# Experts in two halves of the batches, with split matrices kept in DRAM and the first half combined under the second half's tiles

## The reference

```
x = layernorm(x + attention(x))        # 16 heads of 128, 4 groups of K and V, causal
logits = clip(x @ gate_w.T)            # 8 experts
top_w, top_idx = top_k(logits, 2); rw = softmax(top_w)
weighted = (softmax(eaw) @ atoms) * sigmoid(importance)      # 8 x 4096
out = x @ W.T + sum over k of rw[k] * S(weighted[top_idx[k]]) x
x = layernorm(x + out)
```

## Time and profile before

| | us |
|---|---|
| median of 3 runs | 2010.44 (2010.35 to 2011.24) |
| profiled execution, its own time | 2009.37 |
| its span | 2007.8 |
| PE busy | 1830.0 (91%) |
| DVE busy | 1200.9 (60%) |
| POOL busy | 825.7 (41%) |
| ACT busy | 809.5 (40%) |

### The profile page before, as it was taken

One profiled execution on the slowest core, in us unless ns is written; L12 is line 12 of the kernel. 1 busy time (PEld: TensorE's weight loads), 2 busy tenths in 40 slices (PEclk: granted clock), 3 DMA queues, 4 the chain that ended last, 5 costly groups with the idle time before them and its releaser, 6 DMA issues. The chain is left out here.

```text
span 2007.8 us, 35232 instructions
## 1 busy us (share of the span) xinstructions
PE 1830.0 (91%) x9447; PEld 1543.7 (77%) x9448; DVE 1200.9 (60%) x3710; ACT 809.5 (40%) x2038; POOL 825.7 (41%) x1242
## 2 busy tenths in 40 slices
PE   6899999999999999999999999999999824999940
PEld 6788888888888888888888888888888713877730
DVE  4445557775777677667757775777576664222237
ACT  1244434444444444444434443444344353333324
POOL 6266433333342334243324332433333244666633
PEclk9999999999999999999999999999999866999975
DMA  8543353334333433343342334333232152444468
GB/s 306 184 163 132 116 199 107 126 106 139 113 105 105 147 110 120 107 140 110 115 152 94 134 123 145 106 117 123 106 127 74 53 170 93 157 150 153 146 223 358
DMA packets 113038, 278.74 MB, mean 139 GB/s; under 512 B 17809, under 2 KB 28065, under 8 KB 103017
## 3 DMA queue, kind: packets, MB, share of 16 engines
q1 hardware_dynamic: 92128, 229.03, 32.6%
q0 software_dynamic: 20816, 48.73, 7.6%
HBM read 207.00 MB, written 70.72 MB: 138 GB/s over the span
## 5 line engine op out<-in xcount | busy, mean ns | idle before, releaser
L849 POOL TENSOR_SCALAR probs<-probs,row_inv 128x128 f32<-128x128 f32 (+3 forms) x512 | 308.3, 655 | 423.7 <-DVE row_inv L1248 423.1
L1154 ACT ACTIVATE probs<-probs,neg_max 128x512 f32<-128x512 f32 (+3 forms) x512 | 282.2, 553 | 358.4 <-DVE neg_max L1240 356.3
L928 PE MATMUL psum<-xT_hi,w_hi 128*128 128x512 f32 x640 | 253.5, 396 | 6.1 <-PEq L373 3.7
L930 PE MATMUL psum<-xT_hi,w_lo 128*128 128x512 f32 x640 | 251.2, 393 | 0.0
L929 PE MATMUL psum<-xT_lo,w_hi 128*128 128x512 f32 x640 | 250.6, 392 | 0.0
L1240 DVE CUSTOM_DVE_ANT_0 probs<-psum,causal 128x512 f32<-128x512 f32 (+3 forms) x512 | 222.7, 486 | 38.3 <-issue 20.1
L1251 DVE TENSOR_TENSOR pT_lo<-psum,pT_hi 128x512 fp32r<-128x512 f32 (+1 forms) x384 | 206.3, 592 | 21.5 <-ACT pT_hi L1164 21.5
L928 PE MATMUL psum<-wo_hi,oT_hi 128*128 128x512 f32 x512 | 203.3, 397 | 1.5 <-DVE y_acc L1275 0.5
L930 PE MATMUL psum<-wo_hi,oT_lo 128*128 128x512 f32 x512 | 200.4, 391 | 0.0
L929 PE MATMUL psum<-wo_lo,oT_hi 128*128 128x512 f32 x512 | 199.9, 391 | 0.0
L1164 ACT CAST pT_hi<-psum 128x512 fp32r<-128x512 f32 (+1 forms) x384 | 172.4, 526 | 61.0 <-PE psum L955 61.0
(11 more groups left out here) (248 smaller groups left out, 3934.6 us busy)
## 6 DMA issues: line engine op xcount, KB each, us to landing
w_hi<-split_qk_weights SPq DMA_DIRECT2D x140, 256.0 KB, 2.7
w_lo<-split_qk_weights SPq DMA_DIRECT2D x140, 256.0 KB, 2.9
wo_hi<-split_out_weights SPq DMA_DIRECT2D x28, 1024.0 KB, 5.0
wo_lo<-split_out_weights SPq DMA_DIRECT2D x28, 1024.0 KB, 7.0
c_y<-chosen_rows SPq DMA_DIRECT2D x32, 512.0 KB, 9.3
x_in<-in_L_attn_x_dram SPq DMA_DIRECT2D x8, 1024.0 KB, 6.6
expert_weights<-fill_sb SPq DMA_DIRECT2D x4, 2048.0 KB, 9.4
stage<-expert_weights SPq DMA_DIRECT2D x8, 1024.0 KB, 5.3
```

The costliest lines, as they stand in the source:

```text
L849: last = pool.tensor_scalar(p, p, row_inv[:, buf, i:i + 1], 1.0, ALU.mult, ALU.mult)
L928: pe.matmul(dst, hi_s, hi_m, start=start, stop=False)
L930: return pe.matmul(dst, lo_s, hi_m, start=False, stop=stop)
L1154: last = act.activation(probs[:, buf, a:a + w], probs[:, buf, a:a + w], ACT.Exp, bias=neg_max[:, buf, i:i + 1], scale=-1.0, accum_out=row_ ...
```

## The change

- The experts work in two *segments* of four batches (`SEG_B`, `SEG_T` = 16 token tiles), each with its own half of the slot table, its own counts and at most `SEG_TILES` = 39 tiles: 78 tiles in all instead of 72.
- In batches 1 to 4 each iteration scatters twice 128 entries. In batches 5 and 6, two pieces an iteration (16 in all): SP loads 512 KB of `expert_weights`, POOL rounds and subtracts (`split_piece`), and SP writes the hi and lo parts to `split_expert_weights`, expert by expert.
- In batch 7 SP loads the split matrices (2 MB an expert) as parts of attention's buffers come free; the slots of segment 0 are loaded, DVE makes its tables, and POOL fetches the first four tiles. SBUF is laid out by hand (`Space`) so that the buffers may overlap in this way.
- Batch 7's y goes to `attn_residual` like the others, and its four tiles are routed under tiles 0 to 33 of the experts, in seven steps each (`routed`), by the same functions as in attention. Segment 1's tables follow at tiles 29 to 31.
- The 8 pairs of segment 0 are combined under tiles 44 to 76 (`paired`), those of segment 1 behind the last tile. Stores go from SP.
- The gate's rows are loaded by POOL at the end of batch 0. The four iterations of a batch are written out inside the hardware loops, and the 78 tiles without a loop. There are no barriers between attention, experts and combine.

The diff's core:

```diff
+SEGMENTS = 2
+SEG_B = NB // SEGMENTS
+SEG_T = SEG_B * TT
+SEG_TILES = (2 * SEG_T * P + NE * (P - 1)) // P
+JT = SEGMENTS * SEG_TILES
+SCATTER_BATCHES, SPLIT_BATCHES = (1, 5), (5, 7)
...
+    def batch(b, last_kind, route, segment, job):
+        for g in range(HKV):
+            iteration(b, g, b * HKV + g, ("first", "group", "group", last_kind)[g], route, segment, job)
+    batch(0, "batch", False, 0, None)
+    with eng.Fori(*SCATTER_BATCHES) as b:
+        batch(b, "batch", True, 0, "scatter")
+    with eng.Fori(*SPLIT_BATCHES) as b:
+        batch(b, "batch", True, 1, "split")
+    batch(NB - 1, "end", True, 1, "last")
...
+        def load_piece(b, step):
+            src = pieces[bass.ds((b - SPLIT_BATCHES[0]) * 2 + step // PER_C, 1), step % PER_C]
+            sp.dma_start(F.piece_raw[:], src.rearrange("a p n -> (a p) n")).then_inc(s_piece_in, 16)
...
+        def split_piece(b, step):
+            number = piece_number(b, step)
+            raw = F.piece_raw[:].rearrange("p (r e) -> p e r", e=NE)
...
+            pool_round(pool, F.piece_hi[:], raw).then_inc(s_piece, 1)
+            wait_apart(pool, s_piece, 2 * number + 1, s_passed)
+            pool.tensor_tensor(F.piece_lo[:], raw, F.piece_hi[:].bitcast(F32), ALU.subtract).then_inc(s_piece, 1)
...
+                if g == HKV - 1:
+                    sp.wait_ge(s_q, NIT * G)
+                    load_expert(2)
+                    load_expert(3)
+                    sp.wait_ge(s_qk, 3 * NIT * G)
+                    load_expert(4)
+                    sp.wait_ge(s_o, NIT * G)
+                    sp.wait_ge(E.s_tables, 1)
+                    for e in range(5, NE):
+                        load_expert(e)
...
+            if kind != "end":
+                normalize(n + 4, 0)
...
+            if job == "scatter":
+                scatter((it - SCATTER_BATCHES[0] * HKV) * 2 + 1)
...
+            if route:
+                route_place(pool, R, it - TT)
...
+        for j in range(JT):
...
+            if j + GROUP < JT:
+                fetch(pool, R, E, j + GROUP)
+            if j:
+                send(j - 1)
+            tt, step, begun, ranked = routed(j)
+            if ranked and step == 1:
+                route_place(pool, R, tt - 1)
...
+            if begun and step == 2:
+                route_rstd(pool, R, tt)
+            u, step, some = paired(j)
+            if some and step == 2:
+                rstd_of(u)
...
+        add(PAIRS)
+        for v in range(PAIRS_LEFT):
+            u = PAIRS + v
+            spread(u)
+            if v + 1 < PAIRS_LEFT:
+                add(u + 1)
+            variance(u)
+            shift_of(u)
```

More of the change, by code:

```diff
@@ L14 @@
+from collections import namedtuple
 from contextlib import ExitStack
@@ L67, with __init__, __call__ @@
 RAW = HKV
+SCATTER_BATCHES, SPLIT_BATCHES = (1, 5), (5, 7)
+PIECE = P
+PIECES = C * (DM // PIECE)
+PER_C = DM // PIECE
+KB = 1024
+SBUF_FROM, SBUF_TO = 16512, 229344
+class Space:
+    def __init__(self, nc, at, size):
+        self.nc, self.at, self.end = nc, at, at + size
+    def __call__(self, name, shape, dt=F32):
+        size = 4
+        for n in shape[1:]:
+            size *= n
+        tensor = self.nc.alloc_sbuf_tensor_at(name, shape, dt, offset=self.at)
+        self.at += -(-size // 32) * 32
+        assert self.at <= self.end, name
+        return tensor
@@ new lines, in expert_ends, with tiles_behind @@
+def expert_ends(dve, E, t):
+    step = lambda ins: table_step(dve, E, ins)
+    step(dve.tensor_scalar(t.tiles_i[:], t.counts_i[:], P_SHIFT, None, ALU.logical_shift_right))
+    step(dve.tensor_copy(t.tiles[:], t.tiles_i[:]))
+    step(dve.tensor_copy(t.ends[:, 0:1], t.tiles[:, 0:1]))
+    for e in range(1, NE):
+        step(dve.tensor_tensor(t.ends[:, e:e + 1], t.ends[:, e - 1:e], t.tiles[:, e:e + 1], ALU.add))
+def tiles_behind(dve, E, t):
+    step = lambda ins: table_step(dve, E, ins)
+    dve.wait_ge(E.s_tile_at, t.segment + 1)
+    step(dve.tensor_copy(t.tile_at[:], t.tile_at_i[:]))
+    step(dve.tensor_tensor(t.behind[:], t.tile_at[:].unsqueeze(1).broadcast_to([P, NE, SEG_TILES]),
+                           t.ends[:].unsqueeze(2).broadcast_to([P, NE, SEG_TILES]), ALU.is_ge))
+    step(dve.tensor_tensor(t.behind_tiles[:], t.behind[:], t.tiles[:].unsqueeze(2).broadcast_to([P, NE, SEG_TILES]),
+                           ALU.mult))
+    step(dve.tensor_reduce(t.tile_expert[:], t.behind[:].rearrange("p e j -> p j e"), AX.X, ALU.add))
+    step(dve.tensor_reduce(t.tile_start[:], t.behind_tiles[:].rearrange("p e j -> p j e"), AX.X, ALU.add))
@@ L89, in __init__ @@
         self.chosen = sb("route_chosen", [P, 3, NE])
[L90 removed]
+        self.counts = [sb(f"route_counts_{k}", [P, NE]) for k in range(SEGMENTS)]
         self.ranks = sb("route_ranks", [P, NE])
@@ new lines, in build, with _ @@
+        X = experts(sem, s_passed, psum, ident, upper, ones, R, E, tables[1], final, M, y_dram, r_dram, out_rows)
+        with nc.Block() as block:
+            @block.sync
+            def _(sp):
+                M.sync(sp)
+                X.sync(sp)
+            @block.gpsimd
+            def _(pool):
+                M.gpsimd(pool)
+                X.gpsimd(pool)
+            @block.tensor
+            def _(pe):
+                M.tensor(pe)
+                X.tensor(pe)
+            @block.scalar
+            def _(act):
+                M.scalar(act)
+                X.scalar(act)
+            @block.vector
+            def _(dve):
+                M.vector(dve)
+                X.vector(dve)
@@ L310, in route_ranked @@
     wait_apart(dve, R.s_ranks_read, tt + 2, R.passed)
-    step(18, dve.tensor_tensor(R.counts[:], R.counts[:], R.chosen[:, 2], ALU.add))
+    step(18, dve.tensor_tensor(R.counts[segment][:], R.counts[segment][:], R.chosen[:, 2], ALU.add))
     for k in range(2):
```

2130 lines of the change are left out of this document (1029 added, 1101 removed).

## The result

The changed kernel took 1960.4 us (median of 4 runs, 1957.3 to 1967.1) against 2010.4: a ratio of 0.9756, 95% interval 0.9727 to 0.9785. The forecast was 1986, between 1964 and 2006.

What follows compares the result with a forecast made beforehand. It took attention as PE bound and the tiles as POOL bound at 3.42 us each; −13 (attention to last send), −25 (combine) and +14 (attention) sum to −24: span 1984, median 1986 us, range 1964 to 2006.

Steps and rivals of the forecast that it cites:

- A: Stretch from PE's last attention matmul to the last send: 1920.5 against 1933.6 before, so −13 us.
- 73 fetches × 2.12: POOL's row fetches in the tile stage: 155 us of POOL's 278 us of work there.
- When tiles can start: Joint between attention and tiles: expert loads land at 1622, POOL is free for its first send at about 1632.
- B: Combine after the last send: eight pairs left at 4.3 us each, 48.8 against 74.2 us, so −25 us.
- C: What attention pays for setup, scatters, split pieces, tables, clock and batch 7's weights: together +14 us.
- the scatters and the pieces: In attention, doubled scatter-adds in batches 1 to 4 cost +2 us, 16 split pieces in batches 5 and 6 +3.
- the fall of the clock: In attention, one more stretch of lowered PE clock after a wait: +5 us, between 0 and 15.
- The rule on shared SBUF interfaces: GpSimd contends with VectorE's two-SBUF-input instructions; at 2.2 us a piece in attention, pieces cost 35 us instead of 3.
- rival 4: In attention, POOL's pieces hold DVE, 2.2 us each, 35 us lost: 2016 us and up, chance 0.05.
- Rival 1: Attention untouched: scatters, pieces and tables all fall into gaps, 1962 to 1975 us, chance 0.17.
- Rival 2: In the tiles, POOL's placing bursts empty the fetched lead, four clock falls cost +5 each: 1998 to 2008, chance 0.16.
- Rivals 3 and 5: Expert loads not hidden (about 2004 us, chance 0.03); PE at half clock in the tiles (2010 to 2053, chance 0.04).

Runs made afterwards that it cites:

- the nine profiles: Profiles of the changed kernel and variants with the same code in batches 5 and 6; these two batches took 389.0 to 404.4 us.
- the repeat: The changed kernel run once more with nothing changed, for the spread of its executions: 1967.9 us (1960.9 to 1970.5).

## Why the prediction was right and wrong

- **The step that failed** is in A, "73 fetches × 2.12". I took the 2.12 us from a row of the old loop and wrote that the fetch and send of a tile are the same instructions. They are not: the diff replaces the wait and increment between copy and gather by a wait in the gather. Measured it is 1.57 us (1804.91 to the end of L247 at 1806.48), so the fetches cost 115 us instead of 155. POOL's sum falls to 238 us, below PE's 78 × 3.19 = 249: the bound moved to PE. From POOL's rstd (1644.7) to the end of the last send (1915.6) are 271 us, where the sum had 288.5: PE's floor, and some 22 us of start, routing and tail. (The 24 us that the prediction names for routing and pair work are 22.0 by its own terms; the sum does not use the 24.)
- *When tiles can start* held: the loads at 1622 + 15.7 = 1637.7 against 1637.0; POOL free at 1644.7 against 1632 + 15.7 = 1648.
- *B* was right in its reason and 3 us too careful: the wait for rstd is there each time, 0.80 us, but a pair takes 3.8 and not 4.3. In the old pair that I took, 0.56 us lie between the starts of aggregation and of the step behind it (1999.49 to 2000.05), and the shift of the pair before stands in it too (2000.13); in the new one it is 0.27 and no second shift.
- *C* was right in its sum (+15.7 against +14) by offsets, and so by luck: the scatters and the pieces were priced at 5 and cost 11, the fall of the clock at 5 was not needed in this execution. In the nine profiles the pieces alone cost 6 to 21 us (389.0 to 404.4 against 383.1). In the repeat C is +27.5, and A −39: there the two errors cancel, and a median inside the range would have been luck.
- *The rule on shared SBUF interfaces* (the Trainium skill, GPSIMD Engine Reference, Key points) was weighed at 0.2 us a piece, and agrees with the logit of 3.54 us. The row of the setup (2.2 us lost) described the mechanism better than the average of L267 did: an average over 224 instructions beside short POOL instructions says nothing on a long one. The price of rival 4 came to a sixth to three fifths of its 35 us: of the ten logits and two L511 that were held in the changed kernel's first profile, only two show as waits of PE above 1 us.
- *Rival 1* (1962 to 1975) came nearest in number, 2 us off, for a wrong reason: attention was not untouched. *Rival 2* exists with another path; its three long turns are 12.4 us above 3.2 each, 8 in the repeat. *Rivals 3 and 5* did not come; among the tiles the granted clock averages 0.94 up to 1760, where the routing stalls, and 1.00 behind it.

## What to carry to other kernels

When a sum carries a row's duration into new code, every wait inside the step must be compared in the diff, not only its instructions: here an idle time between two instructions, written in the profile as a wait for the own engine, was the largest single item. A bound that is replaced by another one close below it must be given the next engine's floor, measured where that engine never waits. Work moved to an engine that is "half idle" can be priced only after looking at which instructions of the others run beside it and who stands behind it in each queue.

## What was not expected of the hardware

- A wait as an instruction of its own between two POOL instructions costs 0.57 us more (0.84 against 0.27) than the same wait in the instruction that needs it, whether its count is a register's or a constant.
- DVE instructions on SBUF were held to the end of a long POOL instruction, even those of eight elements a partition: L511 took 2.92 us where it takes 0.17, and a logit ended 0.55 us behind POOL's instruction each time.
- Behind the same 2.6 us wait of PE at the same place, the granted clock stayed at 1.00 in five of nine profiles and fell to half in four.
- The cast of a piece (128x1024 read with a step of eight elements) took ACT 2.14 us (median), about POOL's 2.25; the subtraction took DVE 2.08, a third less than POOL's 3.18.
